# Value products of an attention kernel in blocks of two steps, and two row operations on another engine

## The chip, the cores and the metric

The kernel runs on one core of one Trainium2 chip. The metric is the device time of one launch in microseconds (us). The shown time of the kernel before is the median of three runs, 868.2 us (867.61 to 870.95). One more execution was taken by the hardware profiler and took 871.53 us.

## The reference

All tensors are float32. The input is a batch of 8 images of 256 channel rows with 512 tokens each.

```python
x = x + xattn(layernorm(x), ctx, mask, mask, Wq, bq, Wk, bk, Wv, bv)
x = x + ffn(layernorm(x), gate_w, w1, w2)
# xattn: q, k, v = W @ target (or source) + b, 16 heads of 16 channels
dot  = einsum('bhdt,bhds->bhts', q, k) / 4
dot  = mask * dot - (1 - mask) * 1e6
amap = softmax(dot, axis=-1) * mask
out  = einsum('bhts,bhds->bhdt', amap, v)
# ffn: 8 experts, top 2 of softmax(x @ gate_w.T), SwiGLU with inner width 352
out  = sum over the two experts of weight * (silu(g) * u) @ w2.T
```

Layernorm runs over the last axis (512). In the second half a "token" is one of the 2048 channel rows.

## The kernel before, in words

**Units.** The attention works through 16 units of 128 channel rows (half an image, 8 heads). In unit u, TensorE makes the transposed scores of unit u, the plain scores of unit u+1 for its row maxima, the value products of unit u, the projections q of unit u+3 and k of unit u+3, the values v of unit u+1, and, for unit u-2, the transpose (`xT`) of its token rows, their gate logits and their ranks. A unit has eight steps s = 0 to 7, one for each half of the heads and quarter of the keys.

**One step on TensorE** (`unit` in the tensor block): scores of three heads into the three banks `sc` (L1507, bf16), a first "raw" pair into one of two double banks `tile` (L1519, bf16, two products of 512 columns), the fourth head's scores, the value product of the step before (L1545, float32, four products of 32 columns side by side into the bank `pvb`), a second raw pair, and then what the step adds: the values v (L1572) in step 1 of unit 0 and in step 0 of every later unit, the projection q (L1561) and `xT` (L1584) in step 3, the logits (L1594) in step 4, the transpose of the maxima (L1626) in step 6, ranks (L1606 to L1608, between the two raw pairs) and k (L1561) in step 7. Units 0 and 1 have three raw pairs in their first four steps.

**The two slots.** Raw pairs, v, q, k, `xT`, logits, ranks and transposed maxima share the two slots `tiles[0]` and `tiles[1]` in the order of the list `TILES`: before an entry is written, `slot` waits until the entry two before it has been drained. VectorE drains a raw pair by a maximum over 2 x 512 columns (`maximum`, L990) and also drains v, q, k, logits, ranks and the transposed maxima (`split_maxima`, L1003 to L1009). ScalarE drains `xT`.

**ScalarE** takes the exponential of each score bank into `pr[s % 2]` (L843), copies `pvb` out after each half (L817) and the transposed tokens (L824). **VectorE** runs a written order of its own (`unit` in the vector block): the 16 maxima of a unit, and between them the layernorm of the input rows (`batch_stats`, `normalize`, L933), that of the token rows into two copies (`token_normalize`, L945, once for each of the two experts of a row), `reciprocals`, `projection_out`, and the choice of experts (`choose`, six steps, L1017 to L1041; step 0 copies the logits out of their slot, steps 4 and 5 make `sel` and `selb`). **GpSimd** splits q and k into three bf16 parts (`part`, L720 to L728), masks the values (L664), takes the inverse roots (`batch_rstd`, L700 and L702; `token_rstd`, L706 and L708), scatters token rows, and adds the residual (`residual`, L735 and L743). SyncE issues most DMAs.

**After the attention** 36 tiles of 128 routed rows go through the experts on TensorE; eight of them start while the last units' rows are still being made.

The lines of the program that set the order of the products before:

```python
                    if s == 0 and has(u - 1):
                        product(u - 1, 7)
                    if s and has(u):
                        product(u, s - 1)
```

Of the kernel before, what the change touches and what calls it, by code (L numbers as in the profile page):

```python
# [17 lines left out]
P = 128  # L18
# [30 lines left out]
VALUES_AT = 1, 0  # L49
# [72 lines left out]
def fillers(n, s):  # L122

    return ((["v"] if s == VALUES_AT[n > 0] and has(n + 1) else []) + (["q"] if s == 3 and has(n + 3) else [])
            + (["xT"] if s == 3 and has(n - 2) else []) + (["logits"] if s == 4 and has(n - 2) else []))
# [92 lines left out]
def attention(nc, load_expert, x, ctxt, mask, maskc, maskd, wq, wk, wv, bq, bk, bv, gate, ident, ut, iotas,  # L218
# [3 lines left out]
    with st:  # L222
# [14 lines left out]
        mall = sb("mall", [B, T])  # L237
        mrow = sb("mrow", [B, 2, T], BF16)
# [13 lines left out]
        pr = [sb(f"pr{i}", [P, 4, T]) for i in range(2)]  # L252
        ov = sb("ov", [P, 2, T])
        mx = sb("mx", [P, 2, 32])
# [12 lines left out]
        lg = sb("lg", [P, E])  # L267
# [69 lines left out]
        def of(ahead, *names):  # L337
# [15 lines left out]
        rstd = Count(sem("rstd"), of(5, "eps", "pow"))  # L353
# [16 lines left out]
        normed2 = Count(sem("normed2"), of(-2, 0, 1))  # L370
        choice = Count(sem("choice"), of(-2, "v8", "i8", "i8f", "sel", "selb"))
# [12 lines left out]
                 (mall[:, :], mask, mask_in))  # L384
# [265 lines left out]
        def _(pool):  # L650
# [18 lines left out]
            def scatter(u):  # L669
                v = u - 3  # L670
                pool.wait_ge(const_made, MADE)
                pool.wait_ge(ready.sem, ready.at(u - 1, "count" if u == LAST else "ranks"))
                pool.tensor_tensor(before[:, :], before[:, :], selb[:, :], ALU.add).then_inc(summed.sem, 1)
                pool.tensor_copy(xa[:, half(v), :, T + 1:T + 2],
                                 io[:, 88 + v:89 + v].rearrange("p (a o) -> p a o", a=1)
                                 .broadcast_to([P, 2, 1])).then_inc(weight.sem, 1)

                pool.wait_ge(gate_exp.sem, gate_exp.at(u - 1, "e"))
                pool.tensor_scalar(ex1[:, :], ex[:, :], 1.0, None, ALU.add).then_inc(weight.sem, 1)
                pool.wait_ge(weight.sem, weight.at(u, "ex1"))  # L680
# [7 lines left out]
                pool.wait_ge(normed2.sem, normed2.at(u - 1, 1))  # L688

                if (due := routed.at(u - 1, 1)) is not None:  # L690
                    pool.wait_ge(routed.sem, due)
                for j in range(2):
                    pool.indirect_dma_start(
                        routed_d, bass.IndirectOffsetOnAxis(ap=pos[:, half(v), j:j + 1], axis=0),
                        xa[:, half(v), j, :], None).then_inc(routed.sem, 16)

            def batch_rstd(u):
                at = ln[:, half(u + 5), :]
                pool.wait_ge(stats.sem, stats.at(u, "a"))
                pool.tensor_scalar(at[:, 9:10], at[:, 7:8], EPS, None, ALU.add).then_inc(rstd.sem, 1)  # L700
                pool.wait_ge(rstd.sem, rstd.at(u, "eps"))
                pool.tensor_tensor(at[:, 8:9], at[:, 9:10], io[:, 1:2], ALU.pow).then_inc(rstd.sem, 1)  # L702

# [27 lines left out]
            def residual(u):  # L731
# [9 lines left out]
                if (due := normed2.at(u - 1, 1)) is not None:  # L741
                    pool.wait_ge(normed2.sem, due)
# [68 lines left out]
        def _(act):  # L811
# [14 lines left out]

            def gate_weight(u):
# [7 lines left out]
            def unit(u):  # L835
                for s in range(8):
                    for j in range(4):
                        if has(u):
                            act.wait_ge(scored.sem, scored.at(u, (s, j)))

                            if j == 0 and (due := pved.at(u, s, back=2)) is not None:
                                act.wait_ge(pved.sem, due)
                            nc.scalar.activation(pr[s % 2][:, j, :], sc[(32 * u + 4 * s + j) % NSC][:, :],  # L843
# [40 lines left out]
            tile(1, 1)  # L884
            transposed_out(UNITS)
# [3 lines left out]
            tile(4, 0)  # L889
            transposed_out(UNITS + 1)  # L890
# [15 lines left out]
        def _(dve):  # L906
# [29 lines left out]
            def token_normalize(u, j):  # L936
# [6 lines left out]
                if j == 0 and (due := routed.at(u - 1, 1)) is not None:  # L943
                    dve.wait_ge(routed.sem, due)
                dve.tensor_scalar(xa[:, half(v), j, 0:T], x1[:, half(v), :], l2[:, 6:7], l2[:, 8:9],  # L945
                                  ALU.subtract, ALU.mult).then_inc(normed2.sem, 1)

            def token_stats(u, step):
# [3 lines left out]
                if step == 0:  # L952
                    dve.wait_ge(post.sem, post.at(u - 1, "x1"))

                    if (due := normed2.at(u - 1, 1)) is not None:
# [56 lines left out]
            def choose(u, step):  # L1012
# [3 lines left out]
                if step == 0:  # L1016
                    dve.tensor_copy(lg[:, :], tile_of(u, "logits")[:, 0, 0:E]).then_inc(drained.sem, 1)  # L1017
                if step == 1:
                    dve.wait_ge(drained.sem, drained.at(u, "logits"))
# [3 lines left out]
                    dve.max(v8[:, :], lg[:, :]).then_inc(choice.sem, 1)  # L1023
                if step == 2:
                    dve.wait_ge(choice.sem, choice.at(u, "v8"))
                    dve.max_index(i8[:, :], v8[:, :], lg[:, :]).then_inc(choice.sem, 1)
                if step == 3:
                    dve.wait_ge(choice.sem, choice.at(u, "i8"))
# [94 lines left out]
            def second_unit():  # L1123
# [3 lines left out]
                values_out(1)  # L1127

                for m in (3, 4, 5):
                    maximum(1, 2, m)  # L1130
                split_maxima(1, 1, 1)
# [25 lines left out]
            def unit(u):  # L1157
                maximum(u, u + 1, 4)
                normalize(u - 1)
                maximum(u, u + 1, 5)  # L1160
                values_out(u)
# [19 lines left out]
                maximum(u, u + 1, 12)  # L1181
                maximum(u, u + 1, 13)
                choose(u, 0)
                choose(u, 1)
                choose(u, 2)
                choose(u, 3)

                maximum(u, u + 1, 14)
                batch_stats(u, 0)
                maximum(u, u + 1, 15)  # L1190
                batch_stats(u, 1)
                choose(u, 4)
                choose(u, 5)
                if u == TAIL:
                    fetch(0, 0)

                maximum(u, u + 2, 0)
                maximum(u, u + 2, 1)
# [216 lines left out]
            token_normalize(UNITS, 0)  # L1415
            token_normalize(UNITS, 1)
# [29 lines left out]
            token_normalize(UNITS + 1, 0)  # L1446
            token_normalize(UNITS + 1, 1)
# [32 lines left out]
        def _(pe):  # L1480
# [52 lines left out]
            def product(u, s):  # L1533
# [10 lines left out]
                for i in range(4):  # L1544
                    last = nc.tensor.matmul(pvb[32 * i:32 * i + 32, :], vp[half(u)][:, c, 4 * g + i, :],  # L1545
                                            pr[s % 2][:, i, :], start=(c == 0), stop=(c == 3))
# [31 lines left out]
            def transpose_tokens(u):  # L1578
                if not has(u - 2):
                    return  # L1580
                pe.wait_ge(normed2.sem, normed2.at(u, 0))
# [82 lines left out]
            def unit(u):  # L1664
                for s in range(8):
# [18 lines left out]
                    if s == VALUES_AT[u > 0]:  # L1684
# [10 lines left out]
                    if s == 4:  # L1695
# [49 lines left out]
            off = gate(0, 0)  # L1745
            product(TAIL, 7)
# [94 lines left out]
```

## Time and profile before

| what | value |
|---|---|
| median of three runs | 868.2 us |
| the profiled execution | 871.53 us, span 869.7 us |
| TensorE / VectorE / ScalarE / GpSimd busy | 92% / 64% / 37% / 43% of the span |
| mean granted TensorE clock | 0.972 |
| attention, units 0 to 15 | 42.8 to 557 us |
| expert tiles, first eight among the last rows of attention | 557 to 869 us |

A busy TensorE in these rows is not TensorE at its peak: a matmul's record runs from its start to the end of its last column, and records overlap. So the cost of a group is read from the start of the group to the start of the next one. The profiled execution lies 3.3 us above the median, of which 1.8 us lie around its span.

### The profile page before, as it was taken

How to read it: one execution, taken by the hardware profiler on the slowest of the kernel's cores; microseconds unless marked ns; L12 is line 12 of the kernel's file. 1: busy time of each engine (PE TensorE's matmuls, PEld its weight loads, DVE VectorE, ACT ScalarE, POOL GpSimd, SP SyncE). 2: the span in 40 equal slices, each digit the busy share in tenths (PEclk: the TensorE clock that was granted, in tenths of full speed). 3: DMA queues.
4: the chain of work that ended last, by engine and by line, in shares of the span. 5: the costliest groups of instructions: out<-in, count | busy, mean ns of one | idle time of the engine just before them, and what ended most of it. 6: DMA issues, size and time to landing. Idle time of an engine off the chain costs nothing. (4 is left out here: it accounts for less than half of the span.)

```text
span 869.7 us, 13002 instructions
## 1 busy us (share of the span) xinstructions
PE 801.8 (92%) x3757; PEld 365.1 (42%) x3758; DVE 553.6 (64%) x1071; ACT 318.6 (37%) x619; POOL 370.3 (43%) x392
## 2 busy tenths in 40 slices
PE   5888898989999998999989988899999999999993
PEld 2322332333333433433333332365555665665661
DVE  5778887889888887888877874445433333333331
ACT  0035465556565565665655666522000000000000
POOL 7544364556565655655745423334211221211221
PEclk9579999999999999999999999999999999999997
DMA  6745577666766866856845542354648546354332
GB/s 188 231 129 145 172 203 221 200 209 210 231 206 184 264 196 182 257 163 177 244 127 160 172 113 83 94 144 110 152 89 227 133 110 172 65 156 72 72 51 34
DMA packets 84524, 138.02 MB, mean 159 GB/s; under 512 B 14765, under 2 KB 40685, under 8 KB 84474
## 3 DMA queue, kind: packets, MB, share of 16 engines
q1 hardware_dynamic: 68970, 108.65, 41.8%
q0 software_dynamic: 7744, 17.86, 10.7%
q10 hardware_dynamic: 7760, 10.89, 4.5%
q8 instruction: 25, 0.41, 0.2%
q14 instruction: 25, 0.20, 0.1%
HBM read 77.36 MB, written 59.36 MB: 157 GB/s over the span
## 5 line engine op out<-in xcount | busy, mean ns | idle before, releaser
L843 ACT ACTIVATE pr<-sc 128x512 f32<-128x512 f32 x512 | 267.1, 603 | 219.5 <-PE sc L1507 219.3
L990 DVE TENSOR_REDUCE mx<-tile 128x2 f32<-128x1024 f32 x256 | 309.0, 1216 | 55.9 <-PE tile L1519 50.3
L1507 PE MATMUL sc<-qk 100*128 100x512 bf16 x512 | 154.8, 384 | 9.9 <-DMA qk<-mxt 7.2
L1519 PE MATMUL tile<-qk 97*128 97x512 bf16 x496 | 150.9, 388 | 14.0 <-DVE mx L990 7.9
L765 POOL DMA_INDIRECT out_dram<-xin,ids x36 | 56.4, 1566 | 224.0 <-DVE ids L1312 220.0
L1545 PE MATMUL pvb<-pr,vp 128*32 128x512 f32 x1024 | 138.0, 611 | 0.0
L1660 PE MATMUL pvb<-wring,qkf 128*128 (+1 forms) x216 | 98.7, 593 | 1.6 <-DVE qkf L1322 1.6
L720 POOL TENSOR_SCALAR parts<-qkf 128x512 bf16<-128x512 f32 x31 | 46.9, 1512 | 123.3 <-DVE qkf L1074 119.3
L1519 PEld LDWEIGHTS tile<-qk 97*128 97x128 bf16 x496 | 35.0, 98 | 145.6 <-issue 75.7
L1639 PE MATMUL tile<-wring,xh 128*128 x288 | 91.3, 460 | 0.0
L1639 PE MATMUL sc<-wring,xh 128*128 x288 | 91.2, 459 | 0.0
L1507 PEld LDWEIGHTS sc<-qk 100*128 100x128 bf16 x512 | 49.4, 100 | 91.1 <-ACT pr L843 41.2
L1328 DVE TENSOR_SCALAR xin<-pvb,metay 128x512 f32<-128x512 f32 x36 | 27.0, 750 | 68.4 <-PE pvb L1660 68.4
L1639 PEld LDWEIGHTS sc<-wring,xh 128*128 128x128 f32 x288 | 53.1, 190 | 30.9 <-issue 7.7
L1639 PEld LDWEIGHTS tile<-wring,xh 128*128 128x128 f32 x288 | 53.0, 190 | 30.7 <-issue 7.7
L1660 PEld LDWEIGHTS pvb<-wring,qkf 128*128 128x128 f32 (+1 forms) x216 | 41.0, 190 | 43.7 <-issue 36.3
L877 ACT ACTIVATE xh<-sc 128x352 f32<-128x352 f32 x18 | 8.4, 465 | 127.4 <-PE sc L1639 127.4
L877 ACT ACTIVATE xh<-tile 128x352 f32<-128x352 f32 x18 | 8.4, 465 | 124.3 <-PE tile L1639 124.3
L725 POOL TENSOR_SCALAR parts<-rest 128x512 bf16<-128x512 f32 x31 | 46.4, 1498 | 2.7
L735 POOL TENSOR_TENSOR att<-num,rb 128x512 f32<-128x512 f32 x16 | 20.5, 1282 | 58.5 <-DMA rb<-recip_d 58.5
L1320 DVE COPY qkf<-sc 128x256 f32<-128x256 f32 x36 | 15.3, 424 | 46.9 <-PE sc L1650 42.3
L1561 PE MATMUL tile<-xh,wq_s 128*128 128x512 f32 x64 | 33.3, 645 | 10.0 <-DMA bqk<-bq_dram 7.7
(158 smaller groups left out, 789.1 us busy)
## 6 DMA issues: line engine op xcount, KB each, us to landing
qk<-stack_d SPq DMA_DIRECT2D x32, 768.0 KB
stack_d<-parts SPq DMA_DIRECT2D x32, 384.0 KB, 3.1
wring<-w_dram SPq DMA_DIRECT2D x32, 352.0 KB, 7.2
cin<-routed_d ACTq DMA_DIRECT2D x36, 257.0 KB, 3.6
stack_d<-parts SPq DMA_DIRECT2D x32, 256.0 KB, 3.1
pv_d<-ov SPq DMA_DIRECT2D x32, 256.0 KB, 3.4
xin<-x_dram SPq DMA_DIRECT2D x16, 256.0 KB, 5.4
cin<-ctxt_dram SPq DMA_DIRECT2D x8, 512.0 KB, 6.3
```

The source lines that it names most:

```text
L720: pool.tensor_scalar(parts[:, side, 0, :], src, 1.0, None, ALU.mult).then_inc(done.sem, 1)
L725: pool.tensor_scalar(parts[:, side, 1, :], rest[:, side, :], 1.0, None, ALU.mult).then_inc(done.sem, 1)
L765: pool.indirect_dma_start(out, bass.IndirectOffsetOnAxis(ap=ids[:, k, :], axis=0), y[:, k, :], None, compute_op=ALU.add).then_inc(y_added, 16)
L843: nc.scalar.activation(pr[s % 2][:, j, :], sc[(32 * u + 4 * s + j) % NSC][:, :], ACT.Exp, scale=SCALE).then_inc(exped.sem, 1)
L990: dve.tensor_reduce(cols, t[:, :, :], X, ALU.max, negate=True).then_inc(drained.sem, 1)
L1328: dve.tensor_scalar(y[:, k, :], dp, metay[:, k, 0:1], None, ALU.mult).then_inc(y_made, 1)
L1507: nc.tensor.matmul(sc[(32 * u + 4 * s + j) % NSC][:, :], ks[half(u)][0:ALL_ROWS, h, c * P:c * P + P], qs[half(u)][0:ALL_ROWS, h, :], start ...
L1519: last = nc.tensor.matmul(t[:, i, :], qs[half(w)][0:RAW_ROWS, h, c * P:c * P + P], ks[half(w)][0:RAW_ROWS, h, :], start=True, stop=True)
L1545: last = nc.tensor.matmul(pvb[32 * i:32 * i + 32, :], vp[half(u)][:, c, 4 * g + i, :], pr[s % 2][:, i, :], start=(c == 0), stop=(c == 3))
L1561: last = nc.tensor.matmul(t[:, 0, :], weight[:, c, half(w) * P:half(w) * P + P], source[:, parity(w), c, :], start=(c == 0), stop=(c == 1))
L1639: last = nc.tensor.matmul(dst[:, 0:I], xtl[k][:, c, :], wring[:, bass.ds(off + (c * 2 * I + o), I)], start=(c == 0), stop=(c == 3))
L1660: last = nc.tensor.matmul(dp, acT[0:w, c, :], wring[0:w, bass.ds(off + (W1N + c * T), T)], start=(c == 0), stop=(c == len(ICHUNKS) - 1))
```

## The change

The value products of steps s-2 and s-1 are issued together in steps 2, 4 and 6 (and those of steps 6 and 7 in step 0 of the next unit), with a third buffer `pr` for exponentials. The values move to step 1 in all units, the logits from step 4 to step 5. From the third unit on the input rows are normalized on ScalarE, with one more small GpSimd instruction that makes the shift -mean * rstd. VectorE writes one copy of the normalized token rows, ScalarE makes the second from it. The logits are read from their slot by `max` and `max_index`, with no copy. The order of VectorE's work around the maxima is changed. Two small buffers move into `ov`.

```diff
-VALUES_AT = 1, 0
+VALUES_AT = 1
+NPR = 3
...
-            + (["xT"] if s == 3 and has(n - 2) else []) + (["logits"] if s == 4 and has(n - 2) else []))
+            + (["xT"] if s == 3 and has(n - 2) else []) + (["logits"] if s == 5 and has(n - 2) else []))
...
+                pool.wait_ge(rstd.sem, rstd.at(u, "pow"))
+                pool.tensor_scalar(at[:, 10:11], at[:, 6:7], at[:, 8:9], -1.0, ALU.mult, ALU.mult
+                                   ).then_inc(rstd.sem, 1)
...
+            def token_twin(u):
+                act.wait_ge(normed2.sem, normed2.at(u, "n"))
+                nc.scalar.activation(xa[:, half(u), 1, 0:T], xa[:, half(u), 0, 0:T], ACT.Copy
+                                     ).then_inc(twin.sem, 1)
+
+            def normalize(u):
...
+                nc.scalar.activation(xh[:, parity(w), half(w), :], xin[:, half(w), :], ACT.Identity,
+                                     bias=at[:, 10:11], scale=at[:, 8:9]).then_inc(normed.sem, 1)
...
-                            if j == 0 and (due := pved.at(u, s, back=2)) is not None:
+                            if j == 0 and (due := pved.at(u, s, back=NPR)) is not None:
...
+                    if s == 1 and u > 1:
+                        normalize(u - 1)
+                    if s == 3 and has(u - 2):
+                        token_twin(u)
...
                 maximum(u, u + 1, 4)
-                normalize(u - 1)
                 maximum(u, u + 1, 5)
-                values_out(u)
 
                 maximum(u, u + 1, 6)
                 token_stats(u, 0)
                 maximum(u, u + 1, 7)
                 token_stats(u, 1)
+                values_out(u)
 
                 maximum(u, u + 1, 8)
-                token_normalize(u, 0)
+                token_normalize(u)
                 maximum(u, u + 1, 9)
-                token_normalize(u, 1)
...
                     if s == 0 and has(u - 1):
+                        product(u - 1, 6)
                         product(u - 1, 7)
-                    if s and has(u):
+                    if s in (2, 4, 6) and has(u):
+                        product(u, s - 2)
                         product(u, s - 1)
```

On TensorE, steps 2 and 3 of a middle unit read as follows before, from the fourth score of step 2 (`sc`: transposed scores; `tile<-qk`: a raw pair, two rows; `pvb`: a value product).

```order
L1507 MATMUL sc<-qk 128x512 [waits exped]
L1545 MATMUL pvb<-pr,vp 32x512 [waits exped]
L1545 MATMUL pvb<-pr,vp 32x512 x3
L1519 MATMUL tile<-qk 128x512 [waits tile_drained]
L1519 MATMUL tile<-qk 128x512
L1507 MATMUL sc<-qk 128x512 [waits exped] x3
L1519 MATMUL tile<-qk 128x512 [waits tile_drained]
L1519 MATMUL tile<-qk 128x512
L1507 MATMUL sc<-qk 128x512 [waits exped]
L1545 MATMUL pvb<-pr,vp 32x512 [waits exped]
```

In the changed kernel the same place reads:

```order
L1531 MATMUL sc<-qk 128x512 [waits exped]
L1569 MATMUL pvb<-pr,vp 32x512 [waits exped,pv_out,vmade]
L1569 MATMUL pvb<-pr,vp 32x512 x3
L1569 MATMUL pvb<-pr,vp 32x512 [waits exped]
L1569 MATMUL pvb<-pr,vp 32x512 x3
L1543 MATMUL tile<-qk 128x512 [waits tile_drained]
L1543 MATMUL tile<-qk 128x512
L1531 MATMUL sc<-qk 128x512 [waits exped] x3
L1543 MATMUL tile<-qk 128x512 [waits tile_drained]
L1543 MATMUL tile<-qk 128x512
L1531 MATMUL sc<-qk 128x512 [waits exped]
L1543 MATMUL tile<-qk 128x512 [waits tile_drained]
```

Both products now stand in front of the second raw pair of the even step, and none stands between the two raw pairs of the odd step.

On VectorE, the maxima 12 to 15 of a unit and the choice of experts read as follows before.

```order
L990 TENSOR_REDUCE mx<-tile 128x2 [waits tile_ready] x2
L1017 COPY lg<-tile 128x8 [waits tile_ready]
L1023 MAX v<-lg 128x8 [waits gate_exp,tile_drained]
L1026 MAX_INDEX i<-v,lg 128x8 [waits choice]
L1029 CAST i8f<-i 128x8 [waits choice]
L990 TENSOR_REDUCE mx<-tile 128x2 [waits tile_ready]
L918 BN_STATS ln<-xin 128x6 [waits normed,x_in1]
L990 TENSOR_REDUCE mx<-tile 128x2 [waits tile_ready]
L921 BN_AGGR ln<-ln 128x2 [waits stats]
L1032 TENSOR_TENSOR sel<-io,i8f 128x16 [waits choice]
L1041 TENSOR_TENSOR selb<-sel 128x8 [waits summed,choice]
L990 TENSOR_REDUCE mx<-tile 128x2 [waits tile_ready] x2
```

In the changed kernel:

```order
L1020 TENSOR_REDUCE mx<-tile 128x2 [waits tile_ready]
L948 BN_STATS ln<-xin 128x6 [waits normed,x_in1]
L1020 TENSOR_REDUCE mx<-tile 128x2 [waits tile_ready]
L951 BN_AGGR ln<-ln 128x2 [waits stats]
L1020 TENSOR_REDUCE mx<-tile 128x2 [waits tile_ready] x2
L1050 MAX v<-tile 128x8 [waits tile_ready,gate_exp]
L1053 MAX_INDEX i<-v,tile 128x8 [waits tile_ready,choice]
L1056 CAST i8f<-i 128x8 [waits tile_drained]
L1020 TENSOR_REDUCE mx<-tile 128x2 [waits tile_ready]
L1059 TENSOR_TENSOR sel<-io,i8f 128x16 [waits choice]
L1068 TENSOR_TENSOR selb<-sel 128x8 [waits summed,choice]
```

The choice now comes after maximum 15, and its last two steps after the first maximum of step 6.

## Rows read from the trace of the kernel before

**Rows 1.** The page, busy time, and two lines of its 40 slices.

```profile
PE 801.8 (92%) x3757; PEld 365.1 (42%) x3758; DVE 553.6 (64%) x1071; ACT 318.6 (37%) x619; POOL 370.3 (43%) x392
...
PE   5888898989999998999989988899999999999993
...
PEclk9579999999999999999999999999999999999997
```

**Rows 2.** Stretches: bounds, length, busy time (x count) by engine, granted clock, DMA.

```profile
86.80:121.80 35.00, 31.50 (x163) 10.36 (x161) 29.08 (x36) 17.82 (x34) 15.22 (x13) 1.00 0.55 170
...
221.40:252.30 30.90, 30.26 (x170) 11.60 (x170) 27.01 (x44) 18.39 (x36) 19.39 (x22) 1.00 0.73 232
252.30:283.90 31.60, 30.17 (x170) 11.53 (x169) 27.17 (x44) 18.28 (x36) 19.41 (x22) 1.00 0.67 200
...
620.00:869.00 249.00, 234.86 (x839) 141.29 (x839) 79.82 (x233) 13.02 (x28) 46.69 (x30) 0.98 0.48 106
```

**Rows 3.** Timeline of TensorE, one step of unit 9: start, length, what.

```profile
322.26 0.81 PE L1507 MATMUL sc<-qk 100*128 100x512 bf16 x3
322.91 0.60 PE L1519 MATMUL tile<-qk 97*128 97x512 bf16 x2
323.35 0.38 PE L1507 MATMUL sc<-qk 100*128 100x512 bf16 x1
323.66 1.06 PE L1545 MATMUL pvb<-pr,vp 128*32 128x512 f32 x8
324.66 0.60 PE L1519 MATMUL tile<-qk 97*128 97x512 bf16 x2
325.10 0.81 PE L1507 MATMUL sc<-qk 100*128 100x512 bf16 x3
```

**Rows 4.** Timeline of VectorE in the same unit.

```profile
324.80 0.54 DVE L945 TENSOR_SCALAR xa<-x,l 128x512 f32<-128x512 f32 x1
325.30 1.23 DVE L990 TENSOR_REDUCE mx<-tile 128x2 f32<-128x1024 f32 x1
326.44 0.54 DVE L945 TENSOR_SCALAR xa<-x,l 128x512 f32<-128x512 f32 x1
```

**Rows 5.** Timeline of steps 6 and 7 of unit 7, VectorE and TensorE.

```profile
306.66 0.60 PE L1519 MATMUL tile<-qk 97*128 97x512 bf16 x2
...
310.19 0.27 DVE L1003 CAST mxt<-tile 32x128 bf16<-32x128 f32 x1
310.33 0.61 PE L1519 MATMUL tile<-qk 97*128 97x512 bf16 x2 [0.34 <-DVE mx L990]
...
311.39 1.20 DVE L990 TENSOR_REDUCE mx<-tile 128x2 f32<-128x1024 f32 x1
...
312.65 0.60 PE L1519 MATMUL tile<-qk 97*128 97x512 bf16 x2 [0.25 <-DVE mx L990]
...
313.09 1.88 PE L1561 MATMUL tile<-cin,wk_s 128*128 128x512 f32 x4
313.29 1.23 DVE L990 TENSOR_REDUCE mx<-tile 128x2 f32<-128x1024 f32 x1 [0.54 <-PE tile L1519]
...
314.81 0.81 PE L1507 MATMUL sc<-qk 100*128 100x512 bf16 x3
315.46 0.60 PE L1519 MATMUL tile<-qk 97*128 97x512 bf16 x2
```

**Rows 6.** Timeline of unit 6, step 6: GpSimd, VectorE, TensorE.

```profile
275.90 1.28 POOL L735 TENSOR_TENSOR att<-num,rb 128x512 f32<-128x512 f32 x1 [1.81 <-DMA rb<-recip_d]
276.00 1.21 DVE L1041 TENSOR_TENSOR selb<-sel 128x8 bf16<-128x8 f32 x1
...
278.48 0.27 PE L1626 MATMUL tile<-idf,mx 128*32 128x128 f32 x1 [1.09 <-DVE mx L990]
```

**Rows 7.** All instructions of line L1041: shortest, median and longest in ns.

```profile
L1041 DVE TENSOR_TENSOR selb<-sel x16: 166/167/1259, 150.0 to 600.1; 128x8 bf16<-128x8 f32 x16
```

**Rows 8.** Timeline of ScalarE (unit 9), four exponentials of one step.

```profile
322.68 2.07 ACT L843 ACTIVATE pr<-sc 128x512 f32<-128x512 f32 x4 [0.77 <-PE sc L1507]
```

**Rows 9.** Line L843, its table loads: shortest, median, longest in ns.

```profile
L843 ACT ACT_TABLE_LOAD  x1: 1283/1283/1283, 43.5 to 43.5; - x1
```

**Rows 10.** Timeline of GpSimd (unit 9): masked values, then the token rows' inverse root.

```profile
321.56 1.04 POOL L664 TENSOR_TENSOR vp<-vt,mc 128x512 f32<-128x512 f32 x1
323.87 0.22 POOL L706 TENSOR_SCALAR l<-l 128x1 f32<-128x1 f32 x1 [1.26 <-DVE l L960]
324.17 0.57 POOL L708 TENSOR_TENSOR l<-l,io 128x1 f32<-128x1 f32 x1
```

**Rows 11.** Timeline of TensorE in unit 2: a wait for a DMA.

```profile
131.90 0.64 PE L1519 MATMUL tile<-qk 97*128 97x512 bf16 x2 [1.77 <-DMA qk<-mrow_d]
```

More of the change, by code:

```diff
@@ L122, in fillers @@
 def fillers(n, s):
-    return ((["v"] if s == VALUES_AT[n > 0] and has(n + 1) else []) + (["q"] if s == 3 and has(n + 3) else [])
-            + (["xT"] if s == 3 and has(n - 2) else []) + (["logits"] if s == 4 and has(n - 2) else []))
+    return ((["v"] if s == VALUES_AT and has(n + 1) else []) + (["q"] if s == 3 and has(n + 3) else [])
+            + (["xT"] if s == 3 and has(n - 2) else []) + (["logits"] if s == 5 and has(n - 2) else []))
 def tile_events(n):
@@ L251, in attention @@
         vp = [sb(f"vp{i}", [P, 4, UH, 32]) for i in range(2)]
-        pr = [sb(f"pr{i}", [P, 4, T]) for i in range(2)]
+        pr = [sb(f"pr{i}", [P, 4, T]) for i in range(NPR)]
         ov = sb("ov", [P, 2, T])
+        mall = ov[0:B, 0, :]
+        mrow = ov[0:B, 1, :].bitcast(BF16).rearrange("b (s t) -> b s t", s=2)
         mx = sb("mx", [P, 2, 32])
@@ L352, in attention @@
         stats = Count(sem("stats"), of(5, "s", "a"))
-        rstd = Count(sem("rstd"), of(5, "eps", "pow"))
+        rstd = Count(sem("rstd"), of(5, "eps", "pow", "shift"))
         normed = Count(sem("normed"), of(5, "n"))
@@ L369, in attention @@
         rstd2 = Count(sem("rstd2"), of(-2, "eps", "pow"))
-        normed2 = Count(sem("normed2"), of(-2, 0, 1))
-        choice = Count(sem("choice"), of(-2, "v8", "i8", "i8f", "sel", "selb"))
+        normed2 = Count(sem("normed2"), of(-2, "n"))
+        twin = Count(sem("twin"), of(-2, "t"))
+        choice = Count(sem("choice"), of(-2, "v8", "i8f", "sel", "selb"))
         gate_exp = Count(sem("gate_exp"), of(-2, "e"))
@@ L825, in transposed_out @@
                                      .rearrange("p (c o) -> p c o", c=4), ACT.Copy).then_inc(xt_out.sem, 1)
+            def token_twin(u):
[3 more added lines that the diff above has]
+            def normalize(u):
+                w = u + 5
+                if not has(w):
+                    return
+                at = ln[:, half(w), :]
+                act.wait_ge(rstd.sem, rstd.at(u, "shift"))
+                if (due := ready.at(w - 7 + half(w + 1), "q")) is not None:
+                    act.wait_ge(ready.sem, due)
+                nc.scalar.activation(xh[:, parity(w), half(w), :], xin[:, half(w), :], ACT.Identity,
+                                     bias=at[:, 10:11], scale=at[:, 8:9]).then_inc(normed.sem, 1)
             def gate_weight(u):
@@ L934, in normalize, with token_normalize @@
                                   ALU.subtract, ALU.mult).then_inc(normed.sem, 1)
-            def token_normalize(u, j):
+            def token_normalize(u):
                 v = u - 2
@@ L941, in token_normalize @@
                 dve.wait_ge(rstd2.sem, rstd2.at(u, "pow"))
-                if j == 0 and (due := routed.at(u - 1, 1)) is not None:
+                if (due := routed.at(u - 1, 1)) is not None:
                     dve.wait_ge(routed.sem, due)
-                dve.tensor_scalar(xa[:, half(v), j, 0:T], x1[:, half(v), :], l2[:, 6:7], l2[:, 8:9],
+                dve.tensor_scalar(xa[:, half(v), 0, 0:T], x1[:, half(v), :], l2[:, 6:7], l2[:, 8:9],
                                   ALU.subtract, ALU.mult).then_inc(normed2.sem, 1)
@@ L1181, in unit @@
                 maximum(u, u + 1, 12)
+                batch_stats(u, 0)
                 maximum(u, u + 1, 13)
[L1183 to L1186, printed above, removed]
+                batch_stats(u, 1)
                 maximum(u, u + 1, 14)
-                batch_stats(u, 0)
                 maximum(u, u + 1, 15)
-                batch_stats(u, 1)
-                choose(u, 4)
-                choose(u, 5)
+                for step in range(4):
+                    choose(u, step)
                 if u == TAIL:
+                    choose(u, 4)
+                    choose(u, 5)
                     fetch(0, 0)
                 maximum(u, u + 2, 0)
+                if u < TAIL:
+                    choose(u, 4)
+                    choose(u, 5)
                 maximum(u, u + 2, 1)
@@ L1414, in _ @@
             fetch(1, 1)
-            token_normalize(UNITS, 0)
-            token_normalize(UNITS, 1)
+            token_normalize(UNITS)
             multiply(0, 0)
@@ L1444, in _ @@
             note(3, 1)
-            token_normalize(UNITS + 1, 0)
-            token_normalize(UNITS + 1, 1)
+            token_normalize(UNITS + 1)
             finish(3, 1)
@@ L1745, in _ @@
             off = gate(0, 0)
+            product(TAIL, 6)
             product(TAIL, 7)
```

36 lines of the change are left out of this document (17 added, 19 removed).

## The prediction

> **What bounds the kernel now.** I read the page first: TensorE is busy 92% of the span, VectorE 64%, and TensorE's slices stay at 8 or 9 tenths throughout [rows 1]. The average hides two stages, so I cut the span into units. From 620 us on the expert tiles run without VectorE in the way (80 of 249 us busy), and the change touches nothing there [rows 2]. In the attention a unit takes 30.9 to 31.6 us, TensorE is busy for 30.2 of them and VectorE for 27, at full clock (1.00, the 2.4 GHz level) [rows 2]. Both engines are nearly full, so what counts is who waits for whom inside a step, and for that I read the timelines.
>
> One step of TensorE without a wait lasts 2.84 us, from 322.26 to 325.10 [rows 3]: three scores 0.65, a raw pair 0.44, the fourth score with the way into the product 0.31, the product 1.00, a raw pair 0.44. Single scores take 0.65 / 3 = 0.22, so going into the product costs 0.09. A float32 pass of 512 columns takes 0.43 (four in 1.72, from 313.09 to 314.81 [rows 5]); a product is two such passes side by side in four column groups, 0.86, so leaving it costs 0.14. One product thus pays 0.23 for its two borders.
>
> The other limit is the pair of slots. Three intervals set it. A raw pair begins 0.64 before VectorE starts on it (312.65 to 313.29 [rows 5]). A maximum holds VectorE for 1.14 (325.30 to 326.44 [rows 4]). The slot is written again 1.26 after its maximum began (311.39 to 312.65, where TensorE had waited 0.25 [rows 5]). In an ordinary step a slot's maximum is over in time, because the product stands between the two raw pairs. Only steps 6 and 7 wait, 0.34 and 0.25, because the transposed maxima take 1.20 of VectorE between two maxima (310.19 to 311.39 [rows 5]).
>
> **The change, part by part.**
>
> *Blocks of two products, on TensorE's work.* 128 products become 64 blocks. Two passes more inside a block cost 0.86 and one border of 0.23 goes: a block of two lasts 4 x 0.43 + 0.14 = 1.86 after its 0.09. No row shows two products in a row. The ends are 1.72 (no way out at all) and 2.00 (nothing saved); I take 1.86, since float32 passes of the projection follow each other at 0.43 with nothing between [rows 5]. TensorE's own work falls by 64 x 0.23 = 14.7 us.
>
> The Trainium skill (TensorEngine Tiling (Array Packing), Key Properties) says that a change of tiling mode drains TensorE. The 0.09 and 0.14 agree with it, and by that rule alone the sum would be those 14.7 us of gain.
>
> *Blocks of two, on the slots.* Take an even and an odd step, with raw pair A at time 0. Then score and way in 0.31, block 1.86: raw pair B starts at 0.44 + 0.31 + 1.86 = 2.61, and VectorE, which finished A long before, stands idle until 2.61 + 0.64 = 3.25. Now B, C and D follow with no product between them. C's maximum starts at 3.25 + 1.14 = 4.39. D may use B's slot from 3.25 + 1.26 = 4.51 (TensorE would be there at 4.36). The step's filler F (v, q, logits) needs C's slot: 4.39 + 1.26 = 5.65. TensorE would be there at 4.95 and waits 0.70. With three scores 0.65 the pair lasts 6.30 + F, against 2 x 2.84 + F = 5.68 + F before. So each of the first three pairs of a unit loses 0.62: the block saves 0.23 and the two waits cost 0.85. In steps 4 and 5 a 0.09 instruction of `batch_stats` between B and C adds 0.09.
>
> The Trainium skill (TensorEngine Tiling (Array Packing), PSUM Bottleneck) warns that tiling speeds up TensorE but not the emptying of PSUM. Taken alone it would make the loss the two waits, as here.
>
> In steps 6 and 7 B's maximum (3.25) is followed by the transposed maxima: C's maximum starts at 3.25 + 1.14 + 1.20 = 5.59, D at 5.59 + 1.26 = 6.85, then D 0.44, k 1.72, three scores 0.65: 9.66. Before, the same stretch took 8.80, from 306.66 to 315.46 [rows 5]. Loss 0.86.
>
> A full unit loses 3 x 0.62 + 0.09 + 0.86 = 2.8 us. Units 2 to 12 are full: 11 x 2.8 = **+31**.
>
> *Choice of experts moved and shortened.* In some units `selb` takes 1.21 us instead of 0.17: it starts at 276.00 while GpSimd's `att` runs from 275.90 to 277.18, and ends with it; TensorE then waits 1.09 [rows 6, 7]. The same happens to `sel`. That is the difference of 0.7 us between 30.9 and 31.6 [rows 2]. The two steps now stand after A of steps 6 and 7, in the idle time from 1.78 to 3.25, which covers one such delay. Seven units lose it; in five of them it is 0.7, in units 2 and 3 more than 1: **-6**. Dropping the copy of the logits and moving two row operations of 0.5 each off VectorE [rows 4] shortens work that lay in idle time of the new order: nothing more.
>
> *ScalarE.* Two row operations more per unit, 0.49 to 0.60 each (nearest row: four exponentials of this shape in 2.07 [rows 8]). They stand at the end of steps 1 and 3, where TensorE makes v and q, and eight exponentials need 3.9 of a pair's 7 to 9 us: hidden. If that cover went, TensorE would wait up to 1.2 a unit for score banks. The third `pr` buffer removes a wait it would otherwise have.
>
> *GpSimd, SyncE.* The shift is one small instruction (0.22 to 0.57 [rows 10]) and is needed a step and a half later: hidden. The values now reach GpSimd before `token_rstd`, in the next pair's first half microsecond; 1.04 + 0.87 later [rows 10] the token rows can be normalized, about 2.3 after A, before B's maximum at 3.25: hidden with 0.4 to spare, as `token_normalize` itself takes 0.5. The scatter also waits for the copy on ScalarE, a unit ahead. No DMA is added or moved past another; those behind a unit move with it.
>
> *The ends.* Units 0 and 1 have four pairs of steps with six maxima. By the same stepping they cost 8.58 + F against 6.56 + F without waits, +2.0; but unit 1 already takes 35.0 us with VectorE busy for 29.1 [rows 2], so VectorE binds there already: between 0 and 2.0, I take 1.0 each: **+4**. Units 13 and 14 have fewer fillers and raw pairs, +2 and +3: **+5**. Unit 15 has no raw pairs; one product moves from it into the expert stage: 0, within 1 either way. Against this, units that wait for a DMA anyway (1.77 in unit 2 [rows 11]) lose less: between 0 and -6, I take **-4**.
>
> **Sum:** 31 - 6 + 4 + 5 - 4 = +30 us. On the profiled execution, 871.5, that is 901.5; the shown runs have a median 3.3 lower, so I predict 898.
>
> **The rivals.**
>
> *The slots do not bind.* If VectorE kept up in the odd steps, the waits of 0.85 would not come: -14.7 from the borders and -6 from the choice, 868 - 21 = 847. For it: VectorE has 2.0 us less work a unit and four idle microseconds. Against it: the wait of TensorE for the slot after a late maximum is in the rows (0.34, 0.25, 1.09), and nothing shortens the 1.14 between two maxima. It decides where TensorE reaches F later than 1.26 after C's maximum began. Chance 0.11.
>
> *A chain through GpSimd takes over.* If `token_rstd` is later than 3.25 - 0.5 after A, B's maximum slips with it; 1 us in each of 13 units gives 911. The margin is 0.4, and GpSimd's instructions here delay each other (one of VectorE's is delayed by 1.0 in [rows 6]). Chance 0.08.
>
> *ScalarE does not do the new operation for its own length only.* The profile shows a single table load, 1.28, for the exponentials [rows 9]. If the new operation needed another table, two loads a unit, 2.6, would partly stand before exponentials: up to 14 x 2 = 28 more, 926. Copies already mix with exponentials without a load. Chance 0.03.
>
> *The waits come, but smaller,* because a block costs 1.72 and the DMA waits absorb more: +16, 884. Chance 0.12.
>
> **How the numbers follow.** The forecast has 0.62 and the four rivals the rest, 0.04 being left for no change. The time is the forecast's, 898. The range takes in the block's ends (0.14 x 60 = 8 either way), the ends of the first units and of the DMA waits (4 to 6), the smaller-waits case and the GpSimd case: 877 to 912. Half a per cent, 4.3 us, is about what a measurement of this kernel can tell from no change. Faster 0.11, same 0.04, slower 0.62 + 0.08 + 0.03 + 0.12 = 0.85.
>
> **What would show it.** Right: unit lengths of 33 to 34 us in the middle of the attention, with TensorE waiting about 0.7 before v, q and logits in odd steps for VectorE's maximum, 1.2 in step 7; blocks of two lasting 1.86; the 1.2 us `selb` no longer followed by a wait. Wrong: blocks longer than 2.00, waits in front of scores or products for ScalarE, units below 31 us.

## The result, and the profile after

The changed kernel takes 921.3 us (median of four runs, 915.1 to 923.9), the kernel before 869.6 beside it on the same chip: a ratio of 1.059, 95% interval 1.0548 to 1.0632. That is slower by 51.7 us. The forecast was 898, +30, with a range up to 912: the sign came as predicted, the size did not. The profiled execution took 923.9 us (span 922.1), 2.6 above the median.

The page of the kernel after, lines that answer to [rows 1], and two of its costliest groups (busy time, mean ns of one | idle time before them, what ended most of it); then the same two groups of the kernel before:

```profile
PE 820.0 (89%) x3757; PEld 376.1 (41%) x3758; DVE 544.3 (59%) x1029; ACT 335.8 (36%) x645; POOL 373.8 (41%) x408
...
PEclk9589899999999999999999989789999999999998
...
L1020 DVE TENSOR_REDUCE mx<-tile 128x2 f32<-128x1024 f32 x256 | 305.3, 1214 | 93.4 <-PE tile L1543 89.2
...
L1543 PE MATMUL tile<-qk 97*128 97x512 bf16 x496 | 152.2, 390 | 33.1 <-DVE mx L1020 31.2
```

```profile
L990 DVE TENSOR_REDUCE mx<-tile 128x2 f32<-128x1024 f32 x256 | 309.0, 1216 | 55.9 <-PE tile L1519 50.3
...
L1519 PE MATMUL tile<-qk 97*128 97x512 bf16 x496 | 150.9, 388 | 14.0 <-DVE mx L990 7.9
```

No engine became the bound: TensorE's and VectorE's busy shares both fall. The two engines wait for each other. The raw pairs now wait 31.2 us in all for maxima (7.9 before), and the maxima 89.2 us for raw pairs (50.3 before). And the clock line, which before is at 9 tenths from the fourth slice to the last but one, dips again in the fifth slice and reads 8, 7 and 8 in slices near the end of the attention.

The attention in four stretches, first of the kernel before (columns as in [rows 2]: units 0 and 1, 2 to 12, 13 and 14, 15):

```profile
42.83:121.85 79.02, 70.02 (x325) 22.68 (x325) 64.28 (x81) 36.44 (x68) 35.46 (x34) 0.93 0.52 152
121.85:474.67 352.82, 334.57 (x1849) 126.79 (x1850) 295.84 (x479) 201.61 (x396) 208.23 (x231) 1.00 0.68 203
474.67:533.32 58.65, 52.11 (x314) 19.21 (x312) 45.66 (x78) 36.78 (x72) 21.96 (x32) 1.00 0.43 128
533.32:556.13 22.81, 19.56 (x109) 5.61 (x113) 7.28 (x36) 17.01 (x34) 3.31 (x6) 0.93 0.39 117
```

Of the kernel after, the same four stretches, then unit 8 and unit 10 alone:

```profile
42.22:129.41 87.19, 73.45 (x318) 25.59 (x317) 63.92 (x81) 36.41 (x68) 37.34 (x39) 0.88 0.46 138
129.41:510.17 380.76, 339.23 (x1848) 131.91 (x1849) 287.08 (x447) 216.30 (x417) 209.65 (x240) 0.98 0.62 189
510.17:577.21 67.04, 57.02 (x313) 20.64 (x312) 45.70 (x74) 38.02 (x74) 22.09 (x33) 0.91 0.36 110
577.21:607.65 30.44, 26.02 (x114) 7.40 (x114) 6.53 (x34) 17.27 (x35) 5.57 (x7) 0.75 0.28 88
333.32:366.94 33.62, 30.15 (x169) 11.94 (x168) 26.36 (x41) 19.71 (x38) 19.54 (x23) 1.00 0.61 188
403.29:438.61 35.32, 31.85 (x168) 12.13 (x169) 25.70 (x40) 19.70 (x38) 19.57 (x23) 0.95 0.51 152
```

The whole loss lies in the attention: the four stretches grow by 8.2, 27.9, 8.4 and 7.6 us. Unit 8, at full clock, takes 33.62 (units 3 to 7: 33.6 to 34.7), and units 9 to 12, at 0.95 or 0.96, take 35.0 to 36.6.

TensorE of the kernel after, timeline of unit 8: its first two steps, then steps 6 and 7 (the last number is idle time and what ended it):

```profile
333.97 0.60 PE L1543 MATMUL tile<-qk 97*128 97x512 bf16 x2
...
334.71 1.92 PE L1569 MATMUL pvb<-pr,vp 128*32 128x512 f32 x16
336.57 0.61 PE L1543 MATMUL tile<-qk 97*128 97x512 bf16 x2
...
338.49 0.61 PE L1543 MATMUL tile<-qk 97*128 97x512 bf16 x2
339.62 2.05 PE L1596 MATMUL tile<-wv_s,cin 128*128 128x128 f32 x16 [0.52 <-DVE mx L1020]
...
358.06 0.60 PE L1543 MATMUL tile<-qk 97*128 97x512 bf16 x2
...
360.66 0.61 PE L1543 MATMUL tile<-qk 97*128 97x512 bf16 x2
...
364.78 0.60 PE L1543 MATMUL tile<-qk 97*128 97x512 bf16 x2 [1.13 <-DVE mx L1020]
```

VectorE of the kernel after, timeline of the same unit:

```profile
337.21 2.36 DVE L1020 TENSOR_REDUCE mx<-tile 128x2 f32<-128x1024 f32 x2 [1.38 <-PE tile L1543]
...
344.58 0.55 DVE L975 TENSOR_SCALAR xa<-x,l 128x512 f32<-128x512 f32 x1 [0.56 <-POOL l L714]
345.41 2.36 DVE L1020 TENSOR_REDUCE mx<-tile 128x2 f32<-128x1024 f32 x2 [0.28 <-PE tile L1543]
...
360.04 1.16 DVE L1068 TENSOR_TENSOR selb<-sel 128x8 bf16<-128x8 f32 x1
361.31 1.23 DVE L1020 TENSOR_REDUCE mx<-tile 128x2 f32<-128x1024 f32 x1
```

The block lasts 1.86 (334.71 to 336.57). VectorE idles 1.38 until raw pair B has come, then has B and C to drain one after the other, and v, which needs C's slot, stands idle 0.52 for it: the chain of the prediction, step for step.

What the prediction did not have is in the next rows, TensorE of the kernel after in unit 10, from the logits on:

```profile
426.50 1.03 PE L1618 MATMUL tile<-gate_s,xt 128*128 128x8 f32 x8 [0.68 <-DVE mx L1020]
...
428.78 3.62 PE L1569 MATMUL pvb<-pr,vp 128*32 128x512 f32 x16
432.33 0.61 PE L1543 MATMUL tile<-qk 97*128 97x512 bf16 x2
```

The same block that took 1.86 takes 3.55 (428.78 to 432.33), at the lower clock level, 2.3 us after a wait of 0.68 for a maximum. It costs 1.69, and the unit is 35.32 - 33.62 = 1.70 longer than unit 8. The kernel before has two such falls, one in unit 15 (granted 0.93 above) and one behind a wait for a DMA. TensorE of the kernel before, timeline, right after [rows 11]:

```profile
132.90 1.94 PE L1545 MATMUL pvb<-pr,vp 128*32 128x512 f32 x8
```

The stretch from 53 to 620 us, before and after (it takes in the first expert tiles):

```profile
53.00:620.00 567.00, 530.83 (x2833) 209.82 (x2832) 438.54 (x784) 302.21 (x585) 294.27 (x333) 0.99 0.60 177
```

```profile
53.00:620.00 567.00, 499.65 (x2634) 190.18 (x2633) 400.11 (x642) 309.17 (x596) 276.25 (x321) 0.95 0.54 164
```

From 55 us to the end of the attention the granted clock falls to half, the lower level (1.2 GHz), twice before and 12 times after. What a fall costs is estimated here by setting each group of matmuls in it beside the same group at full clock, waits left out: about 3 us before and about 23 us after, good to a microsecond or two.

### The profile page after: what moved, and what is told of

Read it like the earlier page. It is cut to its first block and busy times, and to the rows that moved or that the text cites. A ratio compares the mean times of both kernels' runs of the same rounds, so it can differ in the third digit from the quotient of the medians.

```text
span 922.1 us, 13021 instructions
## 1 busy us (share of the span) xinstructions
PE 820.0 (89%) x3757; PEld 376.1 (41%) x3758; DVE 544.3 (59%) x1029; ACT 335.8 (36%) x645; POOL 373.8 (41%) x408
## 5 line engine op out<-in xcount | busy, mean ns | idle before, releaser
L1020 DVE TENSOR_REDUCE mx<-tile 128x2 f32<-128x1024 f32 x256 | 305.3, 1214 | 93.4 <-PE tile L1543 89.2
L1543 PE MATMUL tile<-qk 97*128 97x512 bf16 x496 | 152.2, 390 | 33.1 <-DVE mx L1020 31.2
L1531 PE MATMUL sc<-qk 100*128 100x512 bf16 x512 | 159.7, 393 | 10.9 <-DMA qk<-mxt 7.5
L1569 PE MATMUL pvb<-pr,vp 128*32 128x512 f32 x1024 | 134.0, 644 | 0.0
L1663 PEld LDWEIGHTS sc<-wring,xh 128*128 128x128 f32 x288 | 53.1, 190 | 30.9 <-issue 7.7
L1569 PEld LDWEIGHTS pvb<-pr,vp 128*32 128x32 f32 x1024 | 28.0, 114 | 62.7 <-issue 43.8
L1585 PE MATMUL tile<-xh,wq_s 128*128 128x512 f32 x64 | 35.9, 689 | 15.1 <-DVE xh L963 8.1
```

What stands on the lines that cost most here:

```text
L1020: dve.tensor_reduce(cols, t[:, :, :], X, ALU.max, negate=True).then_inc(drained.sem, 1)
L1531: nc.tensor.matmul(sc[(32 * u + 4 * s + j) % NSC][:, :], ks[half(u)][0:ALL_ROWS, h, c * P:c * P + P], qs[half(u)][0:ALL_ROWS, h, :], start ...
L1543: last = nc.tensor.matmul(t[:, i, :], qs[half(w)][0:RAW_ROWS, h, c * P:c * P + P], ks[half(w)][0:RAW_ROWS, h, :], start=True, stop=True)
L1585: last = nc.tensor.matmul(t[:, 0, :], weight[:, c, half(w) * P:half(w) * P + P], source[:, parity(w), c, :], start=(c == 0), stop=(c == 1))
L1663: last = nc.tensor.matmul(dst[:, 0:I], xtl[k][:, c, :], wring[:, bass.ds(off + (c * 2 * I + o), I)], start=(c == 0), stop=(c == 3))
```

## The experiments

The theory after the result: about three fifths of the loss are waits for the two slots, which blocks of two cause, and the rest is the clock, which falls because TensorE pauses. Rivals: the row work moved to ScalarE, the new GpSimd instruction, or the choice read from PSUM cost the time; or the blocks cost it by themselves, not through VectorE; or the clock falls for a reason of its own.

**One product per step again.** The changed kernel with its order of value products undone, all else kept.

```diff
+BLOCKED = ()
...
-                    if s in (2, 4, 6) and has(u):
+                    if s and has(u) and u not in BLOCKED:
+                        product(u, s - 1)
+                    if s in (2, 4, 6) and u in BLOCKED:
```

> The changed kernel with one value product per step in all units; all else of the change stays (row work on ScalarE, logits from PSUM, values in step 1, the new order on VectorE). Slots theory: the waits before v, q and logits vanish, a middle unit takes 30.8 to 31.0 us instead of 33.6, the clock stays at 1.00 in the middle units, and the time is 862 to 866, below the kernel before. Rival, that the row work on ScalarE or the later values cost the time: units stay above 33 and the time above 900.

Measured: 869.7 us (twelve runs) against 868.2, ratio 1.0023 (1.0000 to 1.0046). So the blocks make the whole loss, falls of the clock included: two are left, about 3 us, as in the kernel before. Its units 2 to 12, to set beside 352.82 before and 380.76 with blocks:

```profile
122.49:471.55 349.06, 333.24 (x1849) 127.68 (x1850) 283.28 (x447) 213.78 (x417) 209.58 (x240) 1.00 0.67 205
```

The time is some 4 us above what was expected: the rest of the change gains nothing. Step 6 of its unit 5 shows a reason, first GpSimd, then VectorE, then TensorE:

```profile
241.80 1.27 POOL L742 TENSOR_TENSOR att<-num,rb 128x512 f32<-128x512 f32 x1 [2.32 <-DMA rb<-recip_d]
```

```profile
242.39 0.71 DVE L1060 TENSOR_TENSOR sel<-io,i8f 128x16 f32<-128x16 f32 x1
...
243.22 1.22 DVE L1021 TENSOR_REDUCE mx<-tile 128x2 f32<-128x1024 f32 x1
```

```profile
242.36 0.61 PE L1544 MATMUL tile<-qk 97*128 97x512 bf16 x2
...
244.50 0.61 PE L1544 MATMUL tile<-qk 97*128 97x512 bf16 x2 [0.77 <-DVE mx L1021]
```

`sel` ends with GpSimd's `att` again (243.10 and 243.07), the maximum behind it starts 0.86 after its raw pair instead of 0.64, and the next pair waits 0.77 for it. Where the choice is not delayed this wait is 0.56; in six units it is 0.77 to 1.33, 3.2 us more in all. With blocks the delay stood in idle time (the same wait of the changed kernel is 0.56 in all of units 2 to 13); without them the cover is gone, and the forecast gain of 6 us for the choice with it.

**Blocks in the middle units only, and at the ends only.** The same kernel with blocks in units 2 to 13, and with blocks in units 0, 1, 14 and 15.

```diff
-BLOCKED = ()
+BLOCKED = range(2, 14)
```

```diff
-BLOCKED = ()
+BLOCKED = (0, 1, 14, 15)
```

> Blocks of two in units 2 to 13 only, single products in units 0, 1, 14 and 15. Slots theory: units 2 to 13 as in the changed kernel (33.6 and more), the first two and the last two at 44, 35, 28.5 and 23 us: about 893 to 897. If the loss that the prediction left out lies in the middle units, the time is over 905 instead.

> Blocks of two in units 0, 1, 14 and 15 only. Slots theory with the ends undersized in the prediction: 862 + 22 = 884 to 888, of which the prediction had 7. If the ends cost what was predicted: 868 to 872.

Measured: 905.1 us (ratio 1.0424, 1.0364 to 1.0484) and 888.5 (1.0218, 1.0167 to 1.0270). Against the kernel with no block, 35.4 and 18.7; together 54.1, for 51.6 of all blocks. The middle is above its expectation, at the edge of the alternative (905), since there the clock takes part too: seven falls in units 2 to 13, about 11.5 us. The ends cost far more than the +4 of units 0 and 1, the +3 of unit 14 and the 0 of unit 15 that I had put down, and more than half of it is the clock: falls take about 14.5 us in the kernel with blocks at the ends, about 3 in the one with none.

**Maxima of half the length.** The changed kernel, blocks and all, with a shorter drain of each slot.

```diff
-                dve.tensor_reduce(cols, t[:, :, :], X, ALU.max, negate=True
+                dve.tensor_reduce(cols, t[:, :, 0:T // 2], X, ALU.max, negate=True
```

> The changed kernel with each maximum taken over the first 256 of a head's 512 columns (left out: the other half; the maximum only steadies the exponentials). A maximum falls from 1.14 to about 0.6 us. Slots theory: waits before v, q and logits shrink below 0.15, a middle unit takes 30.0 to 30.5, and the time falls by 35 or more, to 868 to 885. If TensorE's own blocks or ScalarE were the cause, nothing changes: 915 to 925.

Measured: 866.5 us, ratio 0.9972 (0.9945 to 0.9999), 55 us less than with whole maxima. So the blocks with their work on TensorE and ScalarE do not make the loss by themselves; the time to empty a slot does. Not all of the 55 us is the blocks', though: units 0 and 1 take 71.0 us here and 78.9 with whole maxima and no block, so short maxima gain there without blocks. Single products with half maxima were not run. TensorE of this kernel, the place before v, where 0.52 of idle time stood:

```profile
307.19 0.60 PE L1543 MATMUL tile<-qk 97*128 97x512 bf16 x2
307.91 2.05 PE L1596 MATMUL tile<-wv_s,cin 128*128 128x128 f32 x16
```

From pair D to v it is 0.72, against 1.13 (338.49 to 339.62) with whole maxima. A pair takes 0.44, so 0.28 is still a wait, more than the 0.15 expected, and the unit before these rows takes 31.1 instead of 30.0 to 30.5.

**Filled pauses.** The changed kernel with three constant bf16 products in each of the four waits of units 2 to 13, into the score bank that is written next.

```diff
+            def spare(u, s):
...
+                for _ in range(3):
+                    nc.tensor.matmul(sc[(32 * w + 4 * r) % NSC][:, :], upper[:, :],
+                                     ones[:, :].rearrange("p (a c) -> p a c", a=1).broadcast_to([P, 4, P]),
+                                     start=True, stop=True)
...
+                    if s in (1, 3, 5):
+                        spare(u, s)
```

> The changed kernel with three constant bf16 products of 512 columns (0.65 us) put into each slot wait of units 2 to 13, before v, q, logits and the last raw pair; their result is overwritten and read by nobody. If the granted clock falls because TensorE pauses there, no fall is left in units 2 to 13 (the changed kernel has five, 1.0 to 2.2 us each) and the time is 912 to 917 against 921. If the clock falls for another reason, the falls stay and the time is unchanged or a few us longer.

Measured: 911.9 us, ratio 1.0493 (1.0460 to 1.0526). More work, 9.4 us less time than the changed kernel, at the lower edge of what was expected. Its windows, units 2 to 13, and its TensorE before v:

```profile
130.11:538.07 407.96, 388.02 (x2153) 153.53 (x2153) 311.98 (x485) 235.22 (x454) 222.87 (x256) 1.00 0.62 187
```

```profile
307.08 0.60 PE L1543 MATMUL tile<-qk 97*128 97x512 bf16 x2
307.52 0.81 PE L1694 MATMUL sc<-ones,upper 128*128 128x512 bf16 x3
308.20 1.05 PE L1596 MATMUL tile<-wv_s,cin 128*128 128x128 f32 x7
```

v starts 1.12 after pair D, as before (1.13): the added products change no wait. But these units now run at a granted clock of 1.00, where the changed kernel had four falls in them and a fifth from the end of unit 13 on. So TensorE's pauses bring the falls. They do not bring one each time: units 2 to 8 of the changed kernel have the same waits at 1.00, and a single wait of 1.91 us in the kernel before (up to 184.38) brought none. The falls left, about 10.5 us, lie in units 0, 1, 14 and 15, where nothing was filled.

**Fillers between the raw pairs.** The changed kernel, blocks kept, with v, q and the logits ahead of pair D from unit 2 on.

```diff
+                    if u > 1:
+                        if s == VALUES_AT:
+                            values(u)
+                        if s == 3:
+                            project(u, 0)
+                        if s == 5:
+                            logits(u)
```

> The changed kernel, blocks of two kept, with v, q and logits between the two raw pairs of the odd step from unit 2 on (VectorE drains them in that order). Same work on every engine. Slots theory by the prediction's stepping: the filler waits for the slot of the pair before the last one (0.15 instead of 0.70), a middle unit loses 1.2 us and falls from 33.6 to about 32.4, and with fewer pauses the clock falls less often: 898 to 908. If only the total work of VectorE counts, 917 to 925.

Measured: 909.7 us, ratio 1.0484 (1.0444 to 1.0525), 11.7 below the changed kernel and above what the waits alone would give. Its windows (units 2 to 13) and its TensorE in unit 8:

```profile
130.12:535.58 405.46, 372.47 (x2009) 149.56 (x2009) 307.74 (x485) 235.32 (x454) 222.96 (x256) 0.96 0.62 188
```

```profile
339.09 0.38 PE L1533 MATMUL sc<-qk 100*128 100x512 bf16 x1
339.49 2.05 PE L1598 MATMUL tile<-wv_s,cin 128*128 128x128 f32 x16
341.38 0.60 PE L1545 MATMUL tile<-qk 97*128 97x512 bf16 x2
...
364.55 0.92 PE L1545 MATMUL tile<-qk 97*128 97x512 bf16 x2 [1.13 <-DVE mx L1022]
365.27 3.30 PE L1587 MATMUL tile<-cin,wk_s 128*128 128x512 f32 x4
368.40 0.81 PE L1533 MATMUL sc<-qk 100*128 100x512 bf16 x3
```

The waits on both sides of v are all but gone: it starts 0.40 after the score (0.18 of it a wait; a score takes 0.22), and pair D follows it at once. So the place of a filler decides the wait. But now the clock falls behind the remaining wait of 1.13 in step 7 in every unit from 4 to 13: in unit 8, k takes 3.13 (365.27 to 368.40) instead of 1.72. Fewer pauses a unit, and more falls: 15, about 27 us. A unit of 34.09 would be about 32.4 without its 1.7. Why the pause of step 7 brings a fall here each time, and in the changed kernel only in some units, is open.

**Row work back on VectorE.** The changed kernel with the normalization of the input rows and the second copy of the token rows on VectorE again.

```diff
-                    if s == 1 and u > 1:
-                        normalize(u - 1)
-                    if s == 3 and has(u - 2):
-                        token_twin(u)
```

> The changed kernel with the two row operations (inputs normalized, second copy of token rows) back on VectorE. Slots theory: they fall mostly into VectorE's idle time behind the first maximum of a pair: 918 to 930. If the move to ScalarE was part of the loss, the time falls below 910.

Measured: 927.8 us, ratio 1.0676 (1.0637 to 1.0714). Not faster, so ScalarE's new work is not where the time went; unit 8, at full clock, takes 33.7 here too.

**A choice that reads one operand from PSUM.** The two largest logits are compared with the logits in their slot; the index, its cast and the two-input operations go. First in the kernel with one product per step, then alone in the kernel before.

```diff
-                    dve.max_index(i8[:, :], v8[:, :], tile_of(u, "logits")[:, 0, 0:E]).then_inc(drained.sem, 1)
...
-                    dve.tensor_tensor(selb[:, :], sel[:, 0, :], sel[:, 1, :], ALU.add).then_inc(choice.sem, 1)
+                    dve.tensor_scalar(selb[:, :], t, v8[:, 1:2], None, ALU.is_ge).then_inc(choice.sem, 1)
+                if step == 3:
+                    dve.tensor_scalar(sel[:, 0, :], t, v8[:, 0:1], None, ALU.is_equal).then_inc(choice.sem, 1)
+                    dve.tensor_scalar(sel[:, 1, :], t, v8[:, 1:2], None, ALU.is_equal).then_inc(drained.sem, 1)
```

> Single products as in the run before, and the choice of experts made from the logits in PSUM: the two masks and their sum are comparisons of the logits with the two largest values, so the index, its conversion and the two instructions with SBUF inputs on VectorE are gone. If the 1.0 to 1.3 us instructions are VectorE waiting for GpSimd over SBUF operands, none is left in the choice, the wait of 0.9 to 1.5 us in step 6 shrinks to about 0.3, and the time is 858 to 863, below the kernel before. If they come from elsewhere, it stays at 866 to 870.

> The kernel before with only the choice of experts changed: masks made by comparing the logits in PSUM with the two largest values. If VectorE's waits for GpSimd in the choice are all that the changed kernel's other parts (row work on ScalarE, new order) helped with, this is as fast as the run with single products and this choice: 863 to 866, none of sel or selb over 0.3 us. If the row work on ScalarE brings something of its own, it stays 2 us or more slower than that run.

Measured: 865.9 us (ratio 0.9960, 0.9939 to 0.9981), above its expectation, and 862.4 (0.9928, 0.9901 to 0.9954), just below. The second is faster than both kernels of this case. Its choice, all 16 units (shortest, median, longest in ns), answers to [rows 7], and a middle unit to [rows 2]:

```profile
L1028 DVE TENSOR_SCALAR selb<-tile,v x16: 225/225/227, 142.3 to 590.8; 128x8 bf16<-128x8 f32 x16
```

```profile
277.05:307.85 30.80, 30.04 (x170) 11.62 (x169) 25.95 (x41) 18.39 (x36) 19.39 (x22) 1.00 0.74 232
```

No instance is stretched (longest 227 ns, before 1259), and the change between 30.9 and 31.6 is gone. But the masks are also made earlier in the unit, mostly before `att` runs, so operand and place changed together. The operand alone is tested where a mask began inside an `att`: twice here (568.23 and 568.36, `att` from 568.20) and twice in the other kernel, each 0.22. What of the gain is due to the place was not separated. That the kernel with the row work on ScalarE is no faster (865.9) says that the rest of the change, the move included, adds nothing to this choice.

## Why the prediction was wrong

The sum of +30 by its stages, in us. The clock's part is what falls cost after, less what they cost before, estimated as above; the rest is the difference:

| units | predicted | measured | of it clock | the rest |
|---|---|---|---|---|
| 0, 1 | +4 | +8.2 | 4.9 | 3.3 |
| 2 to 12 | 31 - 6 - 4 = +21 | +27.9 | 5.0 | 22.9 |
| 13, 14 | +5 | +8.4 | 4.7 | 3.7 |
| 15 | 0 | +7.6 | 5.5 | 2.1 |
| sum | +30 | +52.1 | 20.1 | 32.0 |

**The step that failed** is the first paragraph's "at full clock (1.00, the 2.4 GHz level)", read as if it would stay so. Every term of the sum was worked out at full clock, no rival let it fall, and the range had no room for it: about 20 of the 22 missing microseconds. The rest, 32.0, is close to the forecast 30, in part because misses of 1 to 2 us either way cancel. The waits that I forecast are themselves pauses of TensorE, and the filled pauses show that pauses bring the falls. That is shown for units 2 to 13. Some 15 of the 20 us lie in the other units, where the falls come with the blocks (one product per step, and blocks at the ends only) but no pause was filled. A row that gave a hint was in my hands: the wait of 1.77 in [rows 11] is followed by eight value passes in 1.86 instead of 1.00 (132.90 to 134.76). I used it as a wait that absorbs other waits, and did not read what came after it. It was a hint only, since the wait of 1.09 in [rows 6] brought no fall. The Trainium skill (TensorE: Matmul & The Clock Gate, A second HAM failure mode: psum-queue depth-cycling) tells of a kernel that pauses briefly between groups of matmuls and whose clock swings between its two levels for it. This trace agrees, with its 12 falls, and the rule should have been a rival.

**Blocks on TensorE's work: right.** 1.86 was taken between 1.72 and 2.00; the rows show 1.86.

**Blocks on the slots: right, nearly to the row.** From pair A, in the first two steps of unit 8:

| event | predicted | measured |
|---|---|---|
| raw pair B | 2.61 | 2.60 |
| its maximum | 3.25 | 3.24 |
| raw pair D | 4.51 | 4.52 |
| the filler v | 5.65 | 5.65 |
| steps 6 and 7: last raw pair | 6.85 | 6.72 |

A full unit was to lose 2.8 us; unit 7 before takes 30.83 (283.98 to 314.81), unit 8 after 33.62. (By the order of the units, [rows 3, 4, 8 and 10] lie in unit 8 too, not 9; no number hangs on it.) With half the maxima the loss disappears, as a wait for an emptied slot must.

**Choice of experts: half right.** `selb` still takes 1.16 in unit 8, and the maximum behind it starts 0.65 after its raw pair (360.66 to 361.31), as without a delay [rows 5], so the delay is hidden as I said. But what hides it is the idle time that the blocks make.

**ScalarE, GpSimd and the table: right.** `token_normalize` (344.58 to 345.13) ends 0.28 before B's maximum, where I had put 0.4; with the row work back on VectorE the kernel is not faster.

**The ends: "unit 15 ... 0, within 1 either way" was wrong,** with about 2 of waits and 5.5 of clock. I had priced the product that leaves it, not its order. The block keeps TensorE from scores for 1.86, and ScalarE waits for them; then scores wait for ScalarE. TensorE in unit 15 of the kernel after, around a block, and of the kernel before:

```profile
593.20 0.39 PE L1531 MATMUL sc<-qk 100*128 100x512 bf16 x1 [0.61 <-ACT pr L867]
593.52 1.92 PE L1569 MATMUL pvb<-pr,vp 128*32 128x512 f32 x16
...
596.65 0.39 PE L1531 MATMUL sc<-qk 100*128 100x512 bf16 x1 [0.45 <-ACT pr L867]
```

```profile
548.95 0.39 PE L1507 MATMUL sc<-qk 100*128 100x512 bf16 x1 [0.26 <-ACT pr L843]
```

The waits of 0.61 and 0.45 stand where a step before had 0.26: a wait in front of scores for ScalarE, which the prediction names as a sign of being wrong. No experiment changed this unit alone. Units 0 and 1 (3.3 for 4) and 13 and 14 (3.7 for 5) came near their price, but for the clock.

Of the rivals none was it. That the slots do not bind (847) fell with the waits of unit 8; the smaller waits (884) and the GpSimd chain (911) fell with the timeline above. The new table for ScalarE (926) fell too: ScalarE loads a table six times before and six times after. That 926 and 911 lie nearer to the result than the forecast is chance.

## What to carry to other kernels

When a change batches work on TensorE, step its buffers through the batch: the time that two slots need to empty decides, and where short TensorE work stood between two fills, it was doing service as a spacer. Where the forecast is a set of waits on TensorE, price the clock too, from a row that follows such a wait at the lower level, here about 1.6 us for most falls and 3 for the longest. And a gain that comes from hiding a delay in idle time lasts no longer than that idle time; the choice with an operand from PSUM and an earlier place held by itself.

## What was not expected of the hardware

In the middle units the granted clock fell after pauses of 0.5 to 1.1 us that each unit repeats; the 12 falls of the whole attention cost about 23 us, and filling the pauses of units 2 to 13 with products that nothing reads gave back 9.4 us. Fewer pauses did not mean fewer falls (15, about 27 us, with the fillers between the pairs).

A VectorE instruction of 0.17 us with both inputs in SBUF took up to 1.26 us beside GpSimd [rows 6, 7], ending with GpSimd's instruction; with one input in PSUM and a scalar per row it took 0.23 in all 16 units, and 0.22 in the four masks that began inside `att`. The Trainium skill (SBUF — State Buffer, Who interferes with whom) says that a VectorE instruction with two SBUF inputs contends with a GpSimd instruction that reads SBUF, and that one with at most one SBUF input, outside the modes that use two ports, does not contend with GpSimd; the rows here agree on both, on the second with those four.
